# A later group for the weighted sums' consumers in a graph kernel's edge pass, and a last node update that normalises on ScalarE

## The reference

```python
# layer 0: max over incoming edges, then a small MLP
msgs = z[dst] @ Wd + z[src] @ Ws + edge_weight[:, None] * ww[None, :] + bm
agg = jax.ops.segment_max(msgs, dst, num_segments=n)
x = _layernorm(x + (relu(z @ W1a + agg @ W1b + b1) @ W2 + b2))
# layer 1: softmax-weighted sums over incoming edges
h = x @ node_fc_W + node_fc_b
a = jnp.sum(h[src] * h[dst], axis=-1)
g = sigmoid(...)                      # M = 3 gates of every edge, from edge features
alpha, beta = _seg_softmax(a, dst, n), _seg_softmax(g, dst, n)
s_att = einsum('ed,kdf->ef', h[src], node_att_W)
h_att = segment_sum(alpha[:, None] * s_att, dst) / 3
h_rel = segment_sum(einsum('em,emf->ef', beta, einsum('ed,mdf->emf', h[src], rel_att_W)), dst) / 3
h_red = relu(concat([h_att, h_rel]) @ out_fc_W + out_fc_b)
h_out = where(deg > 0, h_red, h)
x = _layernorm(x + gate * h_out + (1 - gate) * x)
```

## Time and profile before

| | us |
|---|---|
| median of 3 runs (2747.92 to 2776.14) | 2750.39 |
| the profiled execution | 2757.0 |
| its span in the trace | 2755.3 |
| granted TensorE clock, mean over the span | 0.803 |

### The profile page before, as it was taken

How to read it: one execution, slowest core, us unless ns; L and a number is a source line. 1 busy time by engine, 2 the same in 40 slices (tenths; PEclk the granted TensorE clock), 3 DMA queues, 4 the chain that set the end, 5 groups by cost and what they waited for, 6 DMA issues and landing times. The chain is left out here.

```text
span 2755.3 us, 43228 instructions
## 1 busy us (share of the span) xinstructions
PE 1841.2 (67%) x9891; PEld 1141.9 (41%) x9891; DVE 1341.2 (49%) x5207; ACT 1113.2 (40%) x3305; POOL 1654.1 (60%) x1718
## 2 busy tenths in 40 slices
PE   4677777667677775656567776667766667766774
PEld 3222222222222221114356665656655556655674
DVE  4555555554344444324545454445444455444459
ACT  1233333333333333323444444444444444444455
POOL 3756666666677776636445655555555665555535
PEclk7789888988888898777777777777778877787777
DMA  8433333333333333323311212121112122122213
GB/s 232 171 102 124 105 120 107 122 105 124 100 122 103 109 120 108 122 63 93 111 41 51 50 51 52 48 51 52 48 51 52 51 52 52 48 53 51 51 43 99
DMA packets 115983, 235.04 MB, mean 85 GB/s; under 512 B 32909, under 2 KB 68230, under 8 KB 106422
## 3 DMA queue, kind: packets, MB, share of 16 engines
q0 software_dynamic: 52832, 109.39, 16.2%
q1 hardware_dynamic: 56522, 97.21, 9.6%
q10 hardware_dynamic: 6540, 27.42, 2.8%
HBM read 166.01 MB, written 67.89 MB: 85 GB/s over the span
## 5 line engine op out<-in xcount | busy, mean ns | idle before, releaser
L462 POOL DMA_INDIRECT d_region<-d_h,d_region x784 | 747.2, 953 | 552.0 <-issue 238.3
L209 POOL DMA_INDIRECT acc<-d_src_product,b_region x784 | 779.5, 994 | 383.8 <-issue 204.8
L642 PE MATMUL banks<-acc,b_region 64*128 64x512 f32 x1176 | 345.5, 695 | 296.6 <-ACT gate_col L747 159.6
L850 DVE SCALAR_TENSOR_TENSOR acc<-b_region,acc 128x128 f32<-128x128 f32 x784 | 270.4, 345 | 362.9 <-DMA acc<-d_src_product,b_region 333.1
L1570 DVE TENSOR_TENSOR acc<-acc,banks 128x160 f32 x784 | 252.2, 322 | 327.3 <-remote 133.0
L642 PEld LDWEIGHTS banks<-acc,b_region 64*128 64x128 f32 x1176 | 106.2, 204 | 493.2 <-ACT gate_col L747 186.0
L1369 PE MATMUL banks<-d_region 128*128 128x128 f32 x1568 | 303.2, 352 | 9.2 <-issue 9.2
L1372 PE MATMUL banks<-d_region,pick 128*128 128x128 f32 x1568 | 289.2, 344 | 4.7 <-issue 4.5
L1372 PEld LDWEIGHTS banks<-d_region,pick 128*128 128x128 f32 x1568 | 274.0, 260 | 6.6 <-issue 6.5
L1369 PEld LDWEIGHTS banks<-d_region 128*128 128x128 f32 x1568 | 266.3, 255 | 16.4 <-issue 11.0
L861 DVE SCALAR_TENSOR_TENSOR acc<-acc,b_region 128x128 f32<-128x128 f32 x784 | 269.2, 343 | 0.0
(11 more groups left out here) (262 smaller groups left out, 2471.5 us busy)
## 6 DMA issues: line engine op xcount, KB each, us to landing
d_runs<-acc SPq DMA_DIRECT2D x48, 1024.0 KB
acc<-ea ACTq DMA_DIRECT2D x25, 1024.0 KB
acc<-d_src_product,b_region POOLq DMA_INDIRECT x784
d_region<-d_h,d_region POOLq DMA_INDIRECT x784
d_region<-d_rel SPq DMA_DIRECT2D x49, 256.0 KB
hT<-xT SPq DMA_DIRECT2D x7, 448.0 KB, 6.9
d_src_product<-acc SPq DMA_DIRECT2D x7, 448.0 KB, 4.2
acc<-xrow SPq DMA_DIRECT2D x1, 3136.0 KB
```

Of the source, the lines that this page charges most:

```text
L209: pool.indirect_dma_start(self.rows[:, s, j, :], None, d["B"], bass.IndirectOffsetOnAxis(self.idx[:, k:k + 1], 0)).then_inc(self.gathered[ ...
L462: pool.indirect_dma_start(rows[:, s, :], None, table, bass.IndirectOffsetOnAxis(idx[:, s:s + 1], 0)).then_inc(gathered[q], 16)
L642: last = nc.tensor.matmul(bank[4 + n % 2 * 2 + h][:, :], wf[h * DE:(h + 1) * DE, m * P:(m + 1) * P], ea[h * DE:(h + 1) * DE, u % (2 * UC), ...
L850: nc.vector.scalar_tensor_tensor(rows[:, s, j, :], wwb, wgt[:, k:k + 1], rows[:, s, j, :], ALU.mult, ALU.add).then_inc(ch, 1)
```

## The change

Three edits in one diff.

In `phase_edges` every stage except `gate_weights`, `add_windows`, `next_indices`, `rescale` and `sums` takes a group one further ahead, `sums(q)` stands at the head of PE's round, and the prologue has five rounds instead of four. The weight buffers `wts` become four instead of two, and the table `rel` (an edge's place in its window) is kept in BF16 in SBUF and DRAM. In `phase_nodes1` ACT scales only product 0, POOL adds only the bias, DVE joins products 1 to 3, and the normalisation moves to ACT with a bias of minus mean times inverse root, made by a new small operation `shift` on DVE.

```diff
@@ phase_tables
-    t["rel_col"] = sb("rel_col", [P, JP])
+    t["rel_col"] = sb("rel_col", [P, JP], BF16)
...
+            c.add(nc.vector.tensor_copy(short_rel, rel))
             dve.wait_ge(peT, 1)
             c.add(nc.vector.tensor_copy(baseI, bank[0][0:JC, 0:P]))
@@ phase_edges
-        relr = ca(NG * P).rearrange("p (s e) -> p s e", s=NG)
+        relr = ca(NG * P, BF16).rearrange("p (s e) -> p s e", s=NG)
-        wts = [ca(GJ * 4 * W).rearrange("p (j k w) -> p j k w", j=GJ, k=4) for _ in range(2)]
+        wts = [ca(GJ * 4 * W).rearrange("p (j k w) -> p j k w", j=GJ, k=4) for _ in range(4)]
-        LEAD = 4
+        LEAD = 5
@@ PE
             def group(it, q, end):
-                if q + 4 < end:
-                    turn_rows(it, q + 4)
-                if 0 <= q + 3 < end:
-                    scores(it, q + 3)
-                if 0 <= q + 2 < end:
-                    spread(it, q + 2)
-                if 0 <= q + 1 < end:
-                    turn_weights(it, q + 1)
                 if q >= 0:
                     sums(it, q)
+                if q + 5 < end:
+                    turn_rows(it, q + 5)
+                if 0 <= q + 4 < end:
+                    scores(it, q + 4)
+                if 0 <= q + 3 < end:
+                    spread(it, q + 3)
+                if 0 <= q + 2 < end:
+                    turn_weights(it, q + 2)
@@ ACT
             def copy_weights(it, q):
                 act.wait_ge(pt, it * NG + (q + 1 + CREDIT))
-                act.wait_ge(ug, it * NG + (q - 2 + 1 + CREDIT))
+                act.wait_ge(ug, it * NG + (q - 4 + 1 + CREDIT))
...
-                if q + 4 < end:
-                    copy_rows(it, q + 4)
-                    windows(it, q + 4)
-                    penalty(it, q + 4)
-                if 0 <= q + 3 < end:
-                    link_values(it, q + 3)
-                if 0 <= q + 1 < end:
-                    copy_weights(it, q + 1)
+                if q + 5 < end:
+                    copy_rows(it, q + 5)
+                    windows(it, q + 5)
+                    penalty(it, q + 5)
+                if 0 <= q + 4 < end:
+                    link_values(it, q + 4)
+                if 0 <= q + 2 < end:
+                    copy_weights(it, q + 2)
                 if q >= 0:
                     rescale(it, q)
-                if 0 <= q + 2 < end:
-                    weigh(it, q + 2)
+                if 0 <= q + 3 < end:
+                    weigh(it, q + 3)
@@ DVE
             def gate_weights(it, q):
-                dve.wait_ge(ug, it * NG + (q - 2 + 1 + CREDIT))
+                dve.wait_ge(ug, it * NG + (q - 4 + 1 + CREDIT))
...
-                if 0 <= q + 3 < end:
-                    lowest(it, q + 3)
-                    picks(it, q + 3)
+                if 0 <= q + 4 < end:
+                    lowest(it, q + 4)
+                    picks(it, q + 4)
                 if 0 <= q + 1 < end:
                     gate_weights(it, q + 1)
-                if 0 <= q + 2 < end:
-                    references(it, q + 2)
+                if 0 <= q + 3 < end:
+                    references(it, q + 3)
@@ phase_nodes1, POOL
-                    nc.gpsimd.tensor_tensor(sB[c % 2][:, 0:z, :], sB[c % 2][:, 0:z, :],
-                                            ob.unsqueeze(1).to_broadcast([P, z, P]), ALU.add).then_inc(bb, 1)
-                    pool.wait_ge(bb, c + 1)
-                    nc.gpsimd.tensor_tensor(sB[c % 2][:, 0:z, :], sB[c % 2][:, 0:z, :], sA[c % 2][:, 0:z, :], ALU.add
-                                            ).then_inc(bi, 1)
+                    nc.gpsimd.tensor_tensor(sA[c % 2][:, 0:z, :], sA[c % 2][:, 0:z, :],
+                                            ob.unsqueeze(1).to_broadcast([P, z, P]), ALU.add).then_inc(bi, 1)
@@ phase_nodes1, ACT
-                    for k, to in ((0, sA), (1, sB)):
-                        last = nc.scalar.activation(to[c % 2][:, b, :], bank_of(c, b, k), ACT.Copy,
-                                                    scale=rz[:, 4 * c + b, k:k + 1])
+                    last = nc.scalar.activation(sA[c % 2][:, b, :], bank_of(c, b, 0), ACT.Copy,
+                                                scale=rz[:, 4 * c + b, 0:1])
...
+            def norm(c):
+                act.wait_ge(sh, c + 1)
+                for k in range(z):
+                    last = nc.scalar.activation(y[c % 2][:, k, :], v[c % 2][:, k, :], ACT.Identity,
+                                                bias=nmean[c % 2][:, k:k + 1], scale=std[c % 2][:, k:k + 1])
@@ phase_nodes1, DVE
+                for k in range(1, K):
...
+                        last = nc.vector.scalar_tensor_tensor(to[:, b, :], bank_of(c, b, k), rz[:, 4 * c + b, k:k + 1],
+                                                              to[:, b, :], ALU.mult, ALU.add)
-                for k in range(z):
-                    last = nc.vector.tensor_scalar(y[c % 2][:, k, :], v[c % 2][:, k, :], mv[c % 2][:, k, 0:1],
-                                                   std[c % 2][:, k:k + 1], ALU.subtract, ALU.mult)
+                nc.vector.scalar_tensor_tensor(nmean[c % 2][:, 0:z], mv[c % 2][:, 0:z, 0], -1.0, std[c % 2][:, 0:z],
+                                               ALU.mult, ALU.mult).then_inc(sh, 1)
...
                 if 0 <= n + 1 < NC4:
                     join(n + 1)
+                if 0 <= n - 1 < NC4:
+                    shift(n - 1)
                 if 0 <= n < NC4:
                     stats_of(n)
-                if 0 <= n - 1 < NC4:
-                    norm(n - 1)
```

More of the change, by code:

```diff
@@ L433 @@
 CH_TJ = CH_REC + 3 + 2 + JC + 1
-CH_BASE = CH_TJ + 8 + 1
+CH_BASE = CH_TJ + 8 + 2
 def group_bases(nc, ring, eng_type, q, count=GJ):
@@ L1614, in phase_nodes1 @@
         h, x1 = ([v3(cb(G4)) for _ in range(3)] for _ in range(2))
-        sA, sB, r, v = ([v3(ca(G4)) for _ in range(2)] for _ in range(4))
+        sA, r, v = ([v3(ca(G4)) for _ in range(2)] for _ in range(3))
         y = [v3(cb(G4)) for _ in range(2)]
@@ L1618, in phase_nodes1 @@
         mv = [ca(4 * 2).rearrange("p (b s) -> p b s", b=4) for _ in range(2)]
-        std = [ca(4) for _ in range(2)]
+        std, nmean = ([ca(4) for _ in range(2)] for _ in range(2))
         bank = t["psum"]
@@ L1775, in join @@
                 dve.wait_ge(bi, c + 1)
-                done = []
-                for b in range(z):
-                    done.append(h_.add(nc.vector.scalar_tensor_tensor(
-                        sB[c % 2][:, b, :], bank_of(c, b, 2), rz[:, 4 * c + b, 2:3], sB[c % 2][:, b, :],
-                        ALU.mult, ALU.add)))
-                for b in range(z):
-                    h_.wait(done[b])
-                    last = nc.vector.scalar_tensor_tensor(
-                        sA[c % 2][:, b, :], bank_of(c, b, 3), rz[:, 4 * c + b, 3:4], sB[c % 2][:, b, :],
-                        ALU.mult, ALU.add)
+                for k in range(1, K):
+                    to, before = sA[c % 2], done if k > 1 else None
+                    done = []
+                    for b in range(z):
+                        if before:
+                            h_.wait(before[b])
+                        last = nc.vector.scalar_tensor_tensor(to[:, b, :], bank_of(c, b, k), rz[:, 4 * c + b, k:k + 1],
+                                                              to[:, b, :], ALU.mult, ALU.add)
+                        if k < K - 1:
+                            done.append(h_.add(last))
                 last.then_inc(pm, 1)
```

35 lines of the change are left out of this document (20 added, 15 removed).

## The result

| | before | after |
|---|---|---|
| median, same chip (4 and 4 runs) | 2751.8 us | 2901.4 us |
| ratio, 95% interval | | 1.052 [1.048, 1.056] |
| span of the trace | 2755.3 us | 2899.1 us |
| mean clock | 0.803 | 0.788 |

The direction was right, the size was not: +150 us against a forecast of +56. The spans differ by 143.8 us. The page and the trace place them.

The account below looks back on a forecast made before the run. The edge pass was taken to be bound by hand-offs, with no engine full. 2757.0 + 70 - 14 = 2813 us in the profiled execution's time, 2806 us as a median, 2% slower; 8 in 10: 2705 to 2900.

Parts of the forecast that it names:

- Order of TensorE's stages, buffers, BF16: Flat sequence of TensorE's stages unchanged, four weight buffers win or lose nothing, BF16 ring off every chain: 0.
- The closed chain: Edge pass, every group: scores, lowest, picks, gates, sums, rows, scores; 4.6 us at 2.4 GHz, 6.7 at 1.2; +70 us.
- At most 60 more waits at 2.3 us: Edge pass, upper bound from POOL's side: one wait for each group, 196 - 136 = 60 more, +138 us.
- Last node update: Last update: normalisations leave DVE, joins come in, 6.2 to 6.3 us a chunk; together -14 us, bounds -5 and -22.
- Hidden: Rival: in the edge pass the gathers' pace hides the new chain, edges +0; 2736 us, chance 0.24.
- Faster by the relief of DVE: Rival: in the edge pass DVE no longer waits for sums, half of 133.0 us, -67; 2669 us, chance 0.19.
- Clock pulled down: Rival: TensorE's added idle in the edge pass keeps it at half clock, up to +205 us; 2941 us, chance 0.07.

Follow-up runs that it names:

- idx_early: Changed kernel with the copy of the next indices back at its old place, the head of DVE's round: 2808.4 us, 1.021 to the kernel before.
- gates_late: Kernel before with gate_weights(q) in place of gate_weights(q+1), so the gates are made just ahead of the sums: 2933.2 us, 1.066 to before.
- nodes_only: Kernel before with only the new last node update: 2741.1 us, 0.995 to before.
- gates_ahead: Changed kernel with gate_weights one group further ahead (q+2 in place of q+1): 2940.0 us, 1.068 to the kernel before.
- adds_mid: Changed kernel with gates for q+2, index copy heading DVE's round, add_windows(q) ahead of references(q+3): 2867.7 us, 1.041 to before.
- nodes_idx: Kernel before with the new last node update and the index copy one group earlier: 2281.0 us without held signals, 2739.7 us with them, both 0.995.
- idx_late: Kernel before with only the index copy one group later: 2297.0 us, 1.002, without held signals; 2940.0 us, 1.067, when run again with them.
- bf16_buffers: Kernel before, old order and old last update, with the BF16 table and four weight buffers: 2296.1 us, 1.002, without held signals.
- quarter_idx_again: Changed kernel with one gather of four after the first lap and the index copy at its old place: 2628.6 us.
- quarter_before: Kernel before with one gather of four after the first lap of eight groups: 2391.6 us.

## Why the prediction came out half right

- **Order of TensorE's stages, buffers, BF16: 0.** Nearly: 0.2% for BF16 and buffers together, measured without held signals only.
- **The closed chain, +70.** Its place is right: sums wait in nearly every group. With the indices repaired the pass is 61.6 us longer than before (1331.5 against 1269.9), and idx_early with the node update in it took 2808 us, where the forecast for the whole change was 2806. That the numbers meet so closely is partly luck: a group after a fall of the clock took 7.3 us and not 6.7, DVE's 3.1 us at the loop's turn was left out, and gates as late cost 151.5 us of the pass where the additions stay early and join the chain (gates_late), and 246 to 250 with a quarter of the gathers.
- **The step that failed is the list of what the change moves.** It said that `gate_weights`, `add_windows` and `rescale` come one group later. `next_indices` stands in the same list of DVE, between them, and moved too; the diff shows it as unchanged because its own line still says `q`. The section on the change names `next_indices` among the stages that stay; the prediction's working leaves it out. The term was missing. It measures some 90 us in the changed order and 185 us by itself. I read POOL's 50.2 us in 20 waits for it and didn't ask what it becomes one group later.
- **"At most 60 more waits at 2.3 us, +138."** The bound fell: POOL's pauses without issue and its first rose from 136 to 169 in number but from 312.7 to 477.6 us in sum, since 47 of them, those for the copy, last 5.6 us. A bound on the number of waits is none when one of them changes its kind.
- **Last node update, -14.** Right as a difference of kernels: 13.8 us by nodes_only. The stage itself shrank by more, from 111 to 92 us and not to 96, so the term was sized some 5 us short; TensorE's clock, at 0.85 where it was 0.73, goes with that. Two more sizes were off: a normalisation on ACT takes 0.487 us on average (four in a row 1.65) and not 0.33, and DVE is still busy 75.45 us of 92 (forecast: under 75).
- **The rivals.** Hidden: no; even with the indices repaired the kernel is 2.1% slower. Faster by the relief of DVE: the relief came (no row of L1573 waits for sums), its worth did not, against the kernel before; the waits went to `lowest` (L1516, 153.3 us remote, against 44.3 for that line before, L1513). Beside late gates it may be the 90 us between gates_late and idx_early. Clock pulled down: 0.74 against 0.77 in the pass, a small part. With a quarter of the gathers it is a large one, 0.94 to 0.84. The rule of the Trainium skill, page TensorE: Matmul & The Clock Gate, section "HAM oscillation — how this bites in real kernels", that idling between bursts costs the clock, agrees with that direction; it doesn't decide the kernel's own case.

The row of before behind the comparison of L1516 is `DVE d_region L1513 <- remote`, of the same stretch as the earlier trace rows:

```profile
DVE d_region L1513 <- remote: 44.3, 23, 6.0
```

The last update of the changed kernel, which answers to the earlier trace rows: twelve joins, four normalisations and one chunk's products in the timeline. The group row (busy, mean ns | idle before), of 2800 to 2900 us, answers to the earlier trace rows:

```profile
2865.40 3.16 DVE L1793 SCALAR_TENSOR_TENSOR g_region<-banks,g_region 128x128 f32<-128x128 f32 x12
2865.83 1.65 ACT L1749 ACTIVATE hT<-g_region 128x128 f32<-128x128 f32 x4
2868.61 3.84 PE L1688 MATMUL banks<-src_col,acc 128*128 128x128 f32 x32 [1.49 <-DVE g_region L1793]
2875.11 1.25 DVE L1819 SCALAR_TENSOR_TENSOR g_region<-g_region 128x4 f32<-128x4 f32 x1
```

```profile
L1749 ACT ACTIVATE hT<-g_region 128x128 f32<-128x128 f32 x49 | 20.2, 487 | 1.2 <-DVE g_region L1819 0.9
```

The normalisations run beside the joins in 1.65 us; the 4.03 us of the earlier trace rows are gone. The joins took 0.26 us each. What is still stretched on DVE now and then is a small operation (L1819, 0.17 or 1.25 us) and the addition of the residual, with two SBUF inputs (L1805, 0.69 us at 2863.46 and 1.80 at 2868.79), the one that the prediction took to stay exposed. The products of a chunk take 3.84 us where a half-clock chunk took 6.41.

## What to carry to other kernels

When a list of stages is shifted against the others, write out the old and the new flat order of every engine and take each stage of it, those whose line the diff leaves alone too: what kept its index while the rest got another has moved. Ask of every small copy that feeds the engine which sets the pace how many groups of slack it has; here it was under one, and a wait that the profile shows as 50 us was the edge of a cliff of 185. And when an experiment frees one chain, look whether the next one that it reaches was hidden behind it: gates_ahead, adds_mid and nodes_idx mostly changed the name of the wait.

## What had not been expected of the hardware

- **Held signals.** TensorE's signals reach DVE and ACT late while POOL issues gathers in a row: in the pass no remote wait with a quarter of the gathers, 354 us of them on DVE and ACT before with all (133.0, 100.7, 76.4 and 44.3). But at one time three edits (idx_late, bf16_buffers, nodes_idx) had none with all 784 gathers, and the kernel before took 17% less beside them (2292.7 against 2755 us); the part ahead of the pass was shorter there too, with the first gather at 1165 us and not 1343. Gathers in a row are needed for it, by these runs, and are not enough. What else it takes is open.
- **The clock in the last update rose**, 0.73 to 0.85, though only work of DVE, POOL and ACT was changed there. TensorE's wait before the chunk's products that is shown is 1.49 us here and 3.59 us in the earlier trace rows. Over all chunks the waits fell less, from 24.7 to 20.3 us; that they and the clock go together no run separated.
- **The turn of the loop** stands in the trace as a wait for nothing named, 3.08 us on DVE in quarter_idx_again and 0.57 us in quarter_before, with the same loop of eight groups in another order. It isn't the closed chain that makes it long: adds_mid and gates_ahead, with the gates early, show 3.0 to 3.8 us at most of their turns, and gates_late, with them late, shows 0.57. What does is open.
